# The f16 half of the probabilities: a second exp of the scores instead of a copy of the f32 exp

## The reference, cut to what matters

```python
q, k, v = x @ Wq + bq, ctx @ Wk + bk, ctx @ Wv + bv      # 16 heads of 32
scores = q @ k.T / sqrt(32); scores[j >= i] = -1e30      # strictly below the diagonal
attn = softmax(scores); attn[row 0] = 0
x = layer_norm(x + (attn @ v) @ Wo + bo)
out = layer_norm(x + relu(x @ W1 + b1) @ W2 + b2)
```

## Time and profile before

| | us |
|---|---|
| median of 3 runs | 2654.29 (2650.04 to 2656.82) |
| the profiled execution | 2651.14 |
| its span, first to last instruction | 2649.3 |
| PE busy | 2498.2 (94%) |
| DVE busy | 2116.9 (80%) |
| ACT busy | 1629.8 (62%) |
| POOL busy | 1585.5 (60%) |
| mean granted clock of TensorE | 0.989 |

### The profile page before, as it was taken

One profiled execution on the slowest core, in us unless ns is written; L12 is line 12 of the kernel. 1 busy time (PEld: TensorE's weight loads), 2 busy tenths in 40 slices (PEclk: granted clock), 3 DMA queues, 4 the chain that ended last, 5 costly groups with the idle time before them and its releaser, 6 DMA issues.

```text
span 2649.3 us, 62863 instructions
## 1 busy us (share of the span) xinstructions
PE 2498.2 (94%) x22664; PEld 1873.3 (71%) x22664; DVE 2116.9 (80%) x4886; ACT 1629.8 (62%) x2881; POOL 1585.5 (60%) x1721
## 2 busy tenths in 40 slices
PE   4899999999999999879999999999999999999998
PEld 1455555555555555557888888888888888888887
DVE  7999999999999999878767777767767676767675
ACT  2788889899899999886344444343444343444433
POOL 2677777777777777666455555555555555554543
PEclk9999999999999999989999999999999999999999
DMA  5344444443344443345232313222222222222220
GB/s 169 110 117 117 119 114 110 115 109 103 92 103 105 106 106 97 89 140 159 53 69 50 71 46 67 50 69 53 66 56 61 61 57 64 57 65 57 65 57 25
DMA packets 444456, 225.04 MB, mean 85 GB/s; under 512 B 302368, under 2 KB 388192, under 8 KB 444144
## 3 DMA queue, kind: packets, MB, share of 16 engines
q1 hardware_dynamic: 442544, 219.71, 32.5%
q10 hardware_dynamic: 1600, 1.31, 0.2%
HBM read 112.36 MB, written 57.69 MB: 64 GB/s over the span
## 4 chain that ended last, share of the span: by engine, by line
PE 63%; DVE 8%; SPq 8%; POOL 8%; issue 7%; DMA 4%; ACT 1%; ACTq 0%; DVEq 0%; POOLq 0%
PE h_ps L1646 23%; PE acc L1662 20%; POOL prob_lo L495 7%; PE front L1632 6%; PE lin_ps L934 5%; SPq L421 4%; PE max_ps L907 2%; PE st_ps L955 2%; DVE max_ps L886 2%; PE lin_ps L930 1%; PE o_ps L973 1%; SPq L458 1%; SPq L1065 1%; DMA heads<-stage 1%; PE st_ps L986 1%
## 5 line engine op out<-in xcount | busy, mean ns | idle before, releaser
L495 POOL TENSOR_TENSOR prob_lo<-probs,prob_hi 128x512 f16<-128x512 f32 (+1 forms) x768 | 797.8, 1047 | 335.2 <-ACT prob_hi L582 318.5
L1646 PE MATMUL h_ps<-x_halves,W 128*128 128x256 f16 x6144 | 756.2, 273 | 1.8 <-ACT hf L1431 1.7
L1662 PE MATMUL acc<-W,hs 128*128 128x256 f16 x5376 | 669.6, 273 | 0.3 <-DVE hs L1599 0.3
L1646 PEld LDWEIGHTS h_ps<-x_halves,W 128*128 128x128 f16 x6144 | 596.5, 98 | 87.5 <-issue 14.8
L1431 ACT ACTIVATE hf<-h_ps,b1s,scale_evac 128x256 f32<-128x256 f32 x512 | 284.9, 563 | 559.7 <-PE h_ps L1646 557.2
L1662 PEld LDWEIGHTS acc<-W,hs 128*128 128x128 f16 x5376 | 526.0, 98 | 61.4 <-DVE hs L1599 0.6
L1356 POOL TENSOR_TENSOR hf<-hf 128x256 f32<-128x256 f32 x256 | 243.4, 951 | 483.1 <-ACT hf L1431 482.7
L588 ACT ACTIVATE probs<-st_ps,exp_scale 128x512 f32<-128x512 f32 (+1 forms) x768 | 469.3, 611 | 98.2 <-PE st_ps L986 91.6
L886 DVE CUSTOM_DVE_ANT_0 max_ps<-max_ps,mask_q 128x256 f32<-128x256 f32 (+2 forms) x768 | 418.2, 560 | 47.1 <-PE max_ps L907 43.4
L582 ACT ACTIVATE prob_hi<-probs 128x512 f16<-128x512 f32 (+1 forms) x768 | 427.9, 557 | 23.0 <-issue 7.3
L1599 DVE TENSOR_TENSOR hs<-hf,hs 128x896 f16<-128x896 f32 x256 | 282.0, 1121 | 147.8 <-ACT hs L1420 147.7
(11 more groups left out here) (152 smaller groups left out, 3526.1 us busy)
## 6 DMA issues: line engine op xcount, KB each, us to landing
heads<-stage SPq DMA_DIRECT2D x748, 64.0 KB, 2.1
raw_c<-in_cT SPq DMA_DIRECT2D x64, 256.0 KB, 3.4
raw_x<-in_xT SPq DMA_DIRECT2D x64, 256.0 KB, 4.4
o_in<-ctx_rows SPq DMA_DIRECT2D x256, 64.0 KB, 2.5
x_in<-in_x SPq DMA_DIRECT2D x32, 512.0 KB, 4.0
x_rows<-x SPq DMA_DIRECT2D x64, 256.0 KB, 2.1
o_in<-x_rows SPq DMA_DIRECT2D x256, 64.0 KB, 2.4
out<-y SPq DMA_DIRECT2D x32, 512.0 KB, 3.0
```

The source lines that it names most:

```text
L495: pool.tensor_tensor(prob_lo[:, k % 4, 0:w], probs[:, k % PROBS, 0:w], prob_hi[:, k % 4, 0:w], ALU.subtract).then_inc(pl_done, 1)
L1646: last = pe.matmul(h_ps[:, f % 2, 0:T], W1[:, aw, j, f * P:(f + 1) * P], x1_halves[:, item.parity, aa, j, :], start=(j == 0 and m == 0), s ...
L1662: last = pe.matmul(acc_products[:, n, :], hs[:, p % HS, aa, n, :], W2[:, p, aw, n, :], start=(p == 0 and m == 0 and n % 2 == 0), stop=(p = ...
```

## The change

ACT no longer copies `probs` to `prob_hi`. It computes the exp of the scores a second time, with the same bias and scale, directly behind the first, and writes it as f16 to `prob_hi`. The count `exp_done` moves from the first exp to the second, and `ph_done` goes: POOL waits for `exp_done`. The wait for `pv_done` (the buffer of `prob_hi`) now stands in front of the first exp.

```diff
@@ -315,7 +315,6 @@
     rows_loaded = [sem(f"rows_loaded{i}") for i in range(2)]
     st_done = sem("st_done")
     exp_done = sem("exp_done")
-    ph_done = sem("ph_done")
     pl_done = sem("pl_done")
     pv_done = sem("pv_done")
     o_step = sem("o_step")
@@ -490,7 +489,7 @@
             for s in range(SLOTS):
                 for item, k in due(window, s, SLOTS, B, ST_AT, SLOTS):
                     w = ST_WIDTH[k % 3]
-                    wait_for(pool, ph_done, SLOTS, item, k + 1)
+                    wait_for(pool, exp_done, SLOTS, item, k + 1)
                     wait_for(pool, pv_done, SLOTS, item, k + 1 - 4)
                     pool.tensor_tensor(prob_lo[:, k % 4, 0:w], probs[:, k % PROBS, 0:w],
                                        prob_hi[:, k % 4, 0:w], ALU.subtract).then_inc(pl_done, 1)
@@ -575,17 +574,15 @@
 
                             wait_for(act, lin_step, SLOTS, item, -SLOTS)
                             split(item, kind, j)
-                for item, k in due(window, s, SLOTS, B, ST_AT + 1, SLOTS):
-                    w = ST_WIDTH[k % 3]
-                    wait_for(act, exp_done, SLOTS, item, k + 1)
-                    wait_for(act, pv_done, SLOTS, item, k + 1 - 4)
-                    act.activation(prob_hi[:, k % 4, 0:w], probs[:, k % PROBS, 0:w], ACT.Copy).then_inc(ph_done, 1)
                 for item, k in due(window, s, SLOTS, B, ST_AT, SLOTS):
                     w = ST_WIDTH[k % 3]
                     wait_for(act, st_done, SLOTS, item, k + 1)
                     wait_for(act, pl_done, SLOTS, item, k + 1 - PROBS)
+                    wait_for(act, pv_done, SLOTS, item, k + 1 - 4)
                     at = item.n % 3
                     act.activation(probs[:, k % PROBS, 0:w], st_ps[:, k % 2, 0:w], ACT.Exp, bias=PROB_BIAS,
+                                   scale=exp_scale[:, at:at + 1])
+                    act.activation(prob_hi[:, k % 4, 0:w], st_ps[:, k % 2, 0:w], ACT.Exp, bias=PROB_BIAS,
                                    scale=exp_scale[:, at:at + 1]).then_inc(exp_done, 1)
                 yield
```

## The result

| | before | the change |
|---|---|---|
| median, us (20 runs each) | 2653.29 | 2660.26 |
| lowest to highest | 2648.53 to 2658.49 | 2655.27 to 2663.97 |
| ratio of the two, 95% interval | | 1.0026 [1.0018, 1.0033] |
| profiled execution | 2651.14 | 2660.78 |
| its span | 2649.3 | 2659.0 |

The ratio times the median of before is 7 us. That is clear of noise with so many runs, and just inside the 0.3% that the prediction called no change; its forecast was 10 us.

A forecast was written before the change was run, and what follows sets the result against it. No engine full: PE, DVE and ACT nearly so, bound by who waits for whom. Lateness 16 less 4 and 2 gave +10 us, from 2654.3 to 2664 us; range 2644 to 2688, the forecast's own 2662 to 2688.

The forecast's parts named there:

- The sum: Whole kernel: 16 us of lateness less 4 and 2 us of gains for POOL's earlier half, +10 us, 2664 us.
- part 4: POOL gets its f16 half earlier: 4 us less in items 0 to 7, 2 us less in the last item.
- Part 1: ACT's copy becomes an exp: pairs take 1.14 us always, up to 37 us if ACT paced, priced at nothing.
- rival (b): ACT's order was the pace in some stretches, so shorter pairs gain: 2640 us, chance 0.17.
- pointer rule: Skill's 93 ns per pointer operand, making ACT's exp 186 ns dearer, 143 us over 768; prediction said the trace disagrees.
- Part 2: PE gets a score bank back 0.57 us later: taken as nothing, with a bound of 26 us.
- Part 3: ACT's evacuations start later behind the second exp: 32 us of new DVE waiting, half reaching PE, 16 us.
- (a): Rival: DVE waits longer for ACT but PE does not; time 2654 us, within 8 us either way; chance 0.36.
- (c): Rival: ACT becomes the bound, the second exp takes 716 ns, PE waits for banks; 2690 us, chance 0.07.
- One sign of being wrong: ACT's second exp taking over 0.7 us was named as one observation that would show the forecast wrong.

The follow-up runs named there:

- Experiment 1: Kernel before, with the second exp replacing the copy in the copy's old place, behind evacuation and split, and releasing the bank: 0.9981, 5 us under before.
- experiment 9: Kernel before, with the second exp replacing the copy, behind the evacuation but in front of the split: 1.0000 against before.
- experiment 2: Kernel before, with the old copy moved directly behind its exp in the same slot, no second exp: 1.0153, 41 us over before.
- experiment 3: Kernel before, with PE's scores waiting for the copy of two units back instead of its exp, so the bank is released later: 1.0001.
- experiment 4: The change, with all of ACT's evacuations of the projections one slot earlier: 0.9981 against the kernel before, 5 us under it.
- V alone: The change, with only the four V evacuations of an item one slot earlier: 1.0026 against the kernel before, the change's own ratio.
- experiment 10: The change, with only the four q evacuations of an item one slot earlier: 1.0001 against the kernel before.
- experiment 5: Kernel before, copy kept, with ACT's evacuations one slot earlier: 1.0051, 14 us slower.

## Why the prediction was right, point by point

**The sum.** Forecast +10, measured +7 us. It was right in sign and size, and right in the term that decides, the late evacuations. That the number came so close is in part luck: 16 - 4 - 2 was forecast, and the runs have about 12 for the lateness, less about 5 for the shorter pairs that the prediction put at nothing, with nothing shown for the two terms of part 4.

**Part 1** had the pairs right, 1.14 us each, and priced them at nothing. Experiment 1 against before says they are worth about 5 us (both have the evacuations in the same place); experiment 9, with the split behind them, says none. So the term is 0 to 5 us of gain, not nothing for sure. Of rival (b), ACT as the pace, this much is true: in experiment 2, where ACT's pairs are longer, the same lateness costs more.

On the pointer rule of the Trainium skill's page "ScalarE: Activation LUTs", section "What ACT_TABLE_LOAD costs", the prediction read the rows wrongly. The page has 93 ns for each such operand. The trace agrees: the earlier trace rows have 716 for the split, with a scale from memory, against 629 for the copy, 87 ns; the evacuation of stage, with a bias from memory, takes 680 ns on average (0.68) against 591 for V's without, 89 ns. The exp is dearer than the copy by only 54, and by these rows that fits one such operand: its scale is one, its bias is a plain number in the program (`PROB_BIAS`, L164), and it reads PSUM, from which V's plain Copy takes 591 where the copy takes 629 from SBUF. 591 and 89 are 680; the exp takes 683. The function and the type of the result differ too, and no run parts them.

**Part 2** took nothing, and experiment 3 shows nothing even for 53 us of waits in place of 9 (PE and its weight loads together, most of it the loads').

**Part 3** was the term that decides, and was. Its size, 16 us, is 12 in experiments 1 and 4 against the change. Both of its factors were off. DVE's new waiting was to be 32 us; it was 10 (stage 23.4 to 25.1, V 1.4 to 9.7). Half of it was to pass; 12 us of time are more than all of it. What passed was not what DVE's list shows: V alone gives nothing back, q alone 7 us. The step that failed is the way from DVE to PE: I followed the next maxima and mentioned SP's gate in one sentence, without reading SP's waits, nor those of PE's weight loads. Those two views show the lateness (80.5 to 96.3 us, and 96.8 to 132.0); DVE's own list and PE's own row hardly do.

**Part 4** was to give 6 us. Items 0 to 7 got 1.3 us shorter, the last item 2 us longer, and experiment 9 gave nothing for an earlier half. POOL's wait fell by 50 us, and 75 us of waiting for PE's products came beside it. The place itself was rightly seen: a later half there is dear, as the first half of experiment 5 suggests.

**Rivals.** (a), that the lateness is swallowed, is out by experiments 1, 4 and 10, though the measured 7 us lie within its 8. (c), ACT as the bound, did not come: an exp pair holds ACT 1.14 us.

**What was to be seen.** Pairs, ACT's idle time, PE's bank wait and POOL's wait came as told. V's wait did too: over the whole span, from which the prediction's 5.9 us are, it is 14.2 (15 told). DVE's stage wait of 50 us with 60 or more occasions did not come, it was 25.1 with 31, and PE's own waits for maxima rose by 5 us, not 15. ACT's busy time was to rise and stayed (1629.8 to 1628.3 us), as the records of neighbours overlap. One sign of being wrong came: the second exp was not to take over 0.7 us, and its record has 709 ns. It says nothing against the forecast, as its start-to-start time is 0.57 us; the sign was badly chosen (the last section says why).

## What to carry to other kernels

When an engine serves several chains, an edit to one of them is priced by what it moves behind itself in that engine's order, more than by its own length: the same two exps gave +7, 0, -5 and -8 us in four orders. Look for the instruction that other engines' work hangs on most; here it was four of twelve evacuations an item, those whose result SP waits for before its moves, and they are the ones to have early, though not so early that they wait themselves. And do not take the wait that grew for the wait that costs: V's grew sevenfold (1.4 to 9.7 us) and was worth nothing, and bank waits of 53 us, mostly of weight loads, were free.

## What the runs showed of the hardware

An ACT instruction that waits for the result of the one in front of it starts 0.72 us behind it, one that does not 0.57, for the same 512 columns (the medians of 359 exps with their copy behind them before, and of 478 exps with the second exp behind them after, up to 1110 us). A pair of exp and fresh copy thus holds ACT 1.25 us, and a pair that computes the result again from its source 1.14.

In a row of ACT instructions without a wait the recorded durations grow while the starts keep their distance. After the change a wide exp that starts at 698.46 us has 0.69 us, and one at 710.98, in the same unbroken row, 0.85, yet wide ones still start 0.57 behind one another. The ACT rows of this stage have longer mean durations after the change, the untouched stage evacuation too (680 to 708 ns), and so the sum of durations is no measure of ACT's load here. Starts are.
